# Query projection of a two-layer gated cross-attention kernel: all head pairs in couples, products added in their banks

## What is computed

```python
def _L1_xattn_ref(query, key, value, mask, wq, wk, wv, wo):      # 32 query heads of 128, 8 key heads
    q = (query @ wq).reshape(bs, s, N_Q_HEADS, D_K).transpose(0, 2, 1, 3)
    ...
    q = _rope(q)                                                 # x * cos + rot(x) * sin
    ...
    scores = jnp.einsum('bhgqd,bhkd->bhgqk', qg, k) / scale
    ...
    return out @ wo
x = x + jnp.tanh(g_xattn[1]) * _L1_xattn_ref(_layernorm(x, axis=-1), ctx_4096, ctx_4096, mask_BxSxS2_ff1, ...)
```

## Time and profile before

| | |
|---|---|
| median of 3 runs | 2954.3 us (2952.41 to 2957.29) |
| the profiled execution | 2956.85 us, its span 2955.0 us |
| TensorE (PE) | 2920.1 us busy, 99% |
| VectorE (DVE) | 2138.5 us, 72% |
| ScalarE (ACT) | 1392.4 us, 47% |
| GpSimd (POOL) | 1473.9 us, 50% |
| query projection alone, 979 to 1576 us | PE 588.6 of 597 us, DVE 440.0, ACT 167.9, POOL 455.8 |

### The profile page before, as it was taken

One profiled execution on the slowest core, in us unless ns is written; L12 is line 12 of the kernel. 1 busy time (PEld: TensorE's weight loads), 2 busy tenths in 40 slices (PEclk: granted clock), 3 DMA queues, 4 the chain that ended last, 5 costly groups with the idle time before them and its releaser, 6 DMA issues.

```text
span 2955.0 us, 41425 instructions
## 1 busy us (share of the span) xinstructions
PE 2920.1 (99%) x14509; PEld 2449.0 (83%) x14509; DVE 2138.5 (72%) x4912; ACT 1392.4 (47%) x2906; POOL 1473.9 (50%) x1187
## 2 busy tenths in 40 slices
PE   9999999999999999999999999999999999999999
PEld 7888788887688878878888888888888888888887
DVE  8687788887654876688667877676766676766566
ACT  5555566764332422232224666655555555555332
POOL 0000598984322777778776555544444433333254
PEclk9999999999999999999999999999999999999999
DMA  5533221205464654455444777766577556654531
GB/s 200 155 124 116 79 75 70 79 22 179 157 201 151 197 148 113 109 170 140 108 113 143 232 247 233 244 201 211 187 225 237 182 184 193 195 188 153 228 113 73
DMA packets 299546, 471.14 MB, mean 159 GB/s; under 512 B 25725, under 2 KB 138877, under 8 KB 296525
## 3 DMA queue, kind: packets, MB, share of 16 engines
q1 hardware_dynamic: 298620, 467.06, 50.0%
q10 hardware_dynamic: 720, 1.44, 0.1%
HBM read 323.73 MB, written 144.70 MB: 159 GB/s over the span
## 4 chain that ended last, share of the span: by engine, by line
PE 59%; DVE 4%; POOL 1%; DMA 1%; issue 0%; ACT 0%; SPq 0%; POOLq 0%; DVEq 0%; ACTq 0%
PE PB L150 18%; PE PB L151 18%; PE PB L152 18%; PE PB L2432 4%; DVE qp_b L2166 1%; DMA qp_raw<-in_wq 0%; PE PB L2899 0%; DVE PB L2208 0%; DVE qp_r L2214 0%; DVE qp_r L2205 0%; POOL qp_a L2236 0%; POOL at_ql L2608 0%; DVE at_ss L2579 0%; DVE PB L2190 0%; DVE qp_c L2210 0%
## 5 line engine op out<-in xcount | busy, mean ns | idle before, releaser
L2489 ACT ACTIVATE at_ss<-at_ss,at_sm,at_bs 128x256 f32<-128x256 f32 x512 | 301.9, 591 | 325.1 <-DVE at_sm L2569 325.1
L2608 POOL TENSOR_TENSOR at_ql<-at_qf,at_qh 128x512 fp32r<-128x512 f32 x128 | 166.3, 1300 | 530.4 <-ACT at_qh L2473 530.4
L150 PE MATMUL PB<-at_woh,at_ah 128*128 128x512 f32 x1024 | 400.3, 391 | 0.6 <-DVE at_al L2591 0.6
L151 PE MATMUL PB<-at_wol,at_ah 128*128 128x512 f32 x1024 | 399.8, 390 | 0.0
L152 PE MATMUL PB<-at_woh,at_al 128*128 128x512 f32 x1024 | 398.9, 390 | 0.0
L150 PE MATMUL PB<-qp_b,qp_a 128*128 128x512 f32 x896 | 350.8, 391 | 7.8 <-DVE qp_r L2212 3.2
L2599 DVE SCALAR_TENSOR_TENSOR at_xt<-PB,gt,at_xt 128x512 f32<-128x512 f32 x256 | 192.2, 751 | 225.4 <-PE PB L152 224.3
L151 PE MATMUL PB<-qp_b,qp_a 128*128 128x512 f32 x896 | 349.8, 390 | 0.0
L152 PE MATMUL PB<-qp_b,qp_a 128*128 128x512 f32 x896 | 349.7, 390 | 0.0
L2236 POOL TENSOR_TENSOR qp_a<-qp_raw,qp_a 128x512 fp32r<-128x512 f32 x192 | 259.9, 1365 | 99.4 <-ACT qp_a L2128 96.6
L2128 ACT ACTIVATE qp_a<-qp_raw 128x512 fp32r<-128x512 f32 x192 | 113.4, 626 | 292.7 <-POOL qp_raw L2240 162.4
(11 more groups left out here) (327 smaller groups left out, 7854.2 us busy)
## 6 DMA issues: line engine op xcount, KB each, us to landing
at_woh<-wod SPq DMA_DIRECT2D x48, 1024.0 KB, 7.1
at_wol<-wod SPq DMA_DIRECT2D x48, 1024.0 KB, 9.4
qp_raw<-in_wq SPq DMA_DIRECT2D x32, 1024.0 KB, 5.4
qd<-qp_r SPq DMA_DIRECT2D x256, 128.0 KB, 2.5
at_qf<-qd SPq DMA_DIRECT2D x128, 256.0 KB, 3.4
at_rawo<-in_wo SPq DMA_DIRECT2D x32, 512.0 KB, 5.5
wod<-at_woh SPq DMA_DIRECT2D x16, 1024.0 KB, 5.5
wod<-at_wol SPq DMA_DIRECT2D x16, 1024.0 KB, 6.4
```

The lines of the kernel that those rows point to most:

```text
L150: pe.matmul(o, ah, bh, start=start, stop=False, skip_group_check=onto)
L151: pe.matmul(o, ah, bl, start=False, stop=False, skip_group_check=onto)
L2489: m = act.activation(at_ss[s][:, c, :], at_ss[s][:, c, :], ACT.Exp, bias=z[:, 4 + c:5 + c], scale=at_bs[:, qn % 2, 8 + 2 * b + c % 2:9 + 2 ...
L2608: self.pool.tensor_tensor(at_ql[n % 3][:, :], at_qf[n % 2][:, :], asf(at_qh[n % 3][:, :]), ALU.subtract).then_inc(*inc("at_pool", ("q", n)))
```

## The change

All pairs are now in couples. For all pairs but the last couple (`Q_ADDED`) the sums over products are made by TensorE, which adds one product onto the bank of another: M0, M1, M2 and M5 go to one bank (the sum after M5 is sum 5), M3 and M6 to a second, M4 to a third. What is needed of the stages in between is copied out by ScalarE: M0 to `c11`, M0 + M1 to `c12`, M3 to `c22` (`keep`; it was one copy, inside `sum`, and is now three). VectorE has three additions: `c22 = c22 + (M0 + M1 + M2)` is sum 3, `c11 + M4` sum 4, `c12 + (M3 + M6)` sum 6. So a product that adds onto a bank waits for the copy or the sum that reads it before.

The first two copies of the first couple go ahead of the factors 4 and 5 on ScalarE. `x(1,4)` is made, and `x(1,6)` fetched, after the last products of (14,15) and ahead of its turn 1, where it was before M6. `x(1,0)` and `x(1,1)` are fetched in block (4,5). The second piece of the second attention's start (the mask's preparation on VectorE, three GpSimd operations for the first keys) stands ahead of pair 28 and not 29.

```diff
-        Q_BLOCKS = [(0, 1)] + [(n,) for n in range(2, NP - 2)] + [(NP - 2, NP - 1), (NP, NP + 1)] + [(n,) for n in range(NP + 2, LASTP - 1)] + [
-            (LASTP - 1, LASTP)]
+        Q_BLOCKS = [(n, n + 1) for n in range(0, LASTP, 2)]
+        Q_ADDED = Q_COUPLED[:-2]
...
         def qp_bank(pair, i):
             j = qp_at(pair, i)
+            if pair in Q_ADDED:
+                j = qp_at(pair, 0) + {3: 2, 6: 2, 4: 4}.get(i, 0)
...
+        def qp_goes_on(pair, i):
+            return pair in Q_ADDED and i in (1, 2, 5, 6)
...
         def qp_emptied(pair, i):
+            if pair in Q_ADDED and i < 4:
+                return ("qp_dve", ("sum", pair, 3)) if i == 2 else ("qp_act", ("sum", pair, i))
...
+            for pair in Q_BLOCKS[0]:
+                do.keep(pair, 0)
             for k in range(4, NR - 1):
                 do.prepare(*Q_ORDER[k])
...
-                if block[0] in (NP + 2, LASTP - 2):
+                if block[0] in (NP + 2, LASTP - 3):
                     yield
...
                         do.product(pair, i)
+                        if pair > 1 or i:
+                            do.keep(pair, i)
                         do.sum(pair, i)
...
+                    if block[0] == NP - 2 and i == 6:
+                        do.expand(1, 4)
+                        do.fetch_x(1, 6)
                     if i > 4 and block[-1] < LASTP:
...
-                    if block[0] == 3 and i < 2:
+                    if block[0] == 4 and i < 2:
                         do.fetch_x(1, i)
-                    if block[0] == NP - 2 and i:
+                    if block[0] == NP - 2 and i and i != 5:
                         do.expand(1, i - 1)
...
                         m = three(self.pe, BK[b], (w[:, 0, 2 * k + c, :], w[:, 1, 2 * k + c, :]), (x[:, 0, c, :], x[:, 1, c, :]),
-                                  k + c == 0, k + c == 2)
+                                  k + c == 0 and not qp_goes_on(pair, i), k + c == 2, qp_goes_on(pair, i))
...
-            def sum(self, pair, i):
+            def keep(self, pair, i):
                 if i == 0:
                     self.on.wait_ge(*at("qp_pe", ("M", pair, 0)))
...
+                if pair in Q_ADDED and i in (1, 3):
+                    self.on.wait_ge(*at("qp_pe", ("M", pair, i)))
+                    if i == 3 and pair - 2 in Q_ADDED:
+                        self.on.wait_ge(*at("qp_dve", ("q1", pair - 2, 1)))
+                    self.act.activation((qp_c12 if i == 1 else qp_c22)[pair % 2][:, :], BK[qp_bank(pair, i)], ACT.Copy).then_inc(
+                        *inc("qp_act", ("sum", pair, i)))
...
+            def add(self, pair, i):
+
+                dve, on, m = self.dve, self.on, BK[qp_bank(pair, i)]
+                c11, c12, c22 = (a[pair % 2][:, :] for a in (qp_c11, qp_c12, qp_c22))
+                if i == 3:
+                    on.wait_ge(*at("qp_pe", ("M", pair, 2)))
+                    on.wait_ge(*at("qp_act", ("sum", pair, 3)))
+                    dve.tensor_tensor(c22, c22, BK[qp_bank(pair, 2)], ALU.add).then_inc(*inc("qp_dve", ("sum", pair, 3)))
+                if i == 4:
+                    on.wait_ge(*at("qp_pe", ("M", pair, 4)))
+                    on.wait_ge(*at("qp_act", ("sum", pair, 0)))
+                    dve.tensor_tensor(m, c11, m, ALU.add).then_inc(*inc("qp_dve", ("sum", pair, 4)))
+                if i == 6:
+                    on.wait_ge(*at("qp_pe", ("M", pair, 6)))
+                    on.wait_ge(*at("qp_act", ("sum", pair, 1)))
+                    dve.tensor_tensor(m, c12, m, ALU.add).then_inc(*inc("qp_dve", ("sum", pair, 6)))
```

More of the change, by code:

```diff
@@ L2085, in none @@
                 pass
-            fetch_rope = fetch_w = fetch_x = prepare = expand = product = sum = turn = none
+            fetch_rope = fetch_w = fetch_x = prepare = expand = product = keep = sum = turn = none
         class QpTensor(Queries):
@@ L2172, in sum @@
                 c11, c12, c21 = (a[pair % 2][:, :] for a in (qp_c11, qp_c12, qp_c21))
+                if pair in Q_ADDED:
+                    self.add(pair, i)
+                    return
                 if i == 0:
@@ L2198, in turn @@
                     on.wait_ge(*at("qp_rope", 1))
-                    on.wait_ge(*at("qp_dve", ("sum", pair, (5, 6)[tn])))
+                    if pair in Q_ADDED and tn == 0:
+                        on.wait_ge(*at("qp_pe", ("M", pair, 5)))
+                        on.wait_ge(*at("qp_dve", ("sum", pair, 4)))
+                    else:
+                        on.wait_ge(*at("qp_dve", ("sum", pair, (5, 6)[tn])))
                     if n > 1:
```

## The result

The changed kernel takes **2963.47 us** (median of 7 runs, 2961.02 to 2965.53) where the kernel before took 2955.14 on the same chip (7 runs, 2951.95 to 2957.38): a ratio of 1.0029, 95% interval 1.0019 to 1.0038. It is 8.3 us slower, where +1.7 was forecast. That is 1.5 us outside the forecast's own range (2949 to 2962), inside the wider one that counts half of a rival (2945 to 2966), and beyond the 0.2% that can be told from no change.

A forecast was written before the change was run, and what follows sets the result against it. TensorE, busy 99% of the span, was taken to bound the kernel, with at most 11.7 us to win. 3.5 - 4.2 + 9.2 - 7.5 + 0.7 = +1.7 us on 2954.3 gave 2956.0 us, range 2949 to 2962.

The forecast's parts named there:

- half of a rival: The wider range for the whole kernel with half of either rival on the forecast's side: 2945 to 2966 us.
- first couple: Pairs 0 to 3: waits for ScalarE's copies and pair 3's weights, 3.5 us with restarts where 4.2 went before.
- steady couples: Couples away from the making of activations: ScalarE's copy of M0 comes in time, so no wait, 0.
- second activations: Pairs 16 and 17: ScalarE's copies late behind the second activations' factors, 9.2 us where 7.5 went before.
- start of the attention: Four GpSimd operations that PE waits for at 1577.62, beside pair 29's turn 1: +0.7 us, bounds -0.2 and +1.5.
- slack 3.1: In steady couples, ScalarE's copy of M0 was put 3.1 us ahead of when it is wanted.
- the rival of stalls at every couple: ScalarE's copy of M0 late at each of 13 changes of couple: 2965, or 2978 with 1 us more each; chance 0.14.
- into a place where POOL was idle 47.9 of 195 us: The second attention's prepared pieces, moved one pair earlier on GpSimd and VectorE, were to cost nothing.
- VectorE: Whole kernel: 83 us of additions gone, 57 us of slower turns added, so about 26 us less busy.
- ScalarE: Whole kernel: 60 copies of 0.60 us, so 36 us more busy.
- The first rival: Waits at both activation places go: half gone wins 5.3 us (2949), all gone 11.7 (2942.5); chance 0.2.
- the rival's half case: Half of the forecast's waits at the two activation places gone: 5.3 us won, 2949 us.

The follow-up runs named there:

- e12: The kernel before, nothing added and its own blocks, with only the fastest version's order of the second activations: 2953.70 us, ratio 0.9999.
- e2: The changed kernel with sum 3 of pairs 28 and 29 in free PSUM banks in place of SBUF: 2959.29 us, ratio 1.0013.
- e3: The changed kernel with the second piece of the attention's start ahead of pair 26 in place of 28: 2960.74 us, ratio 1.0014.
- e11: The changed kernel with sum 3 in banks, the attention's piece ahead of pair 26, and the copies and turns 0 ahead of the second activations' factors: 2950.95 us, 0.9981.
- couples-alone kernel: The kernel before with all pairs in couples and the attention's piece ahead of pair 28, nothing added in banks: 2966.08 us, ratio 1.0032.

## Why the prediction was right or wrong

By place, the lost time in us (idle, 0.26 for each restart, and the slow stretch behind, counted over 4 us as in the prediction):

| | before | forecast | measured |
|---|---|---|---|
| first couple | 4.2 | 3.5 | 1.25 + 1.64 + 0.46 + 0.8 = 4.1 |
| steady couples | 0 | 0 | 0 |
| second activations | 7.5 | 9.2 | 1.07 + 4.26 + 1.52 + 0.8 + 1.3 = 8.9 |
| start of the attention, over before | | +0.7 | +3.0, and +1.5 behind it |
| change in all | | +1.7 | +5.8 |

- **First couple.** The copy of M0 + M1 was 1.25 late (1.3 forecast, 1.6 with the restart), at the place forecast. The weights of pair 3 were 1.64 late, where I had 0.7, and the copy behind them 0.46 instead of 0.8. Right, 0.6 short. That 4.2 went in exchange holds for the profiled execution only, as e12 shows.
- **Steady couples, slack 3.1.** Right: no wait in 190 us. ScalarE had waited 1.87 us for M0 before its copy at 1104.04, and that copy had another 2.72 - 0.60 to spare, so the slack was 4.0; the rival of stalls at every couple has nothing for it.

```profile
1104.04 0.60 ACT L2171 ACTIVATE qp_c<-PB 128x512 f32<-128x512 f32 x1 [1.87 <-PE PB L152]
```

- **Second activations.** Right in mechanism: ScalarE's copies behind `expand`, with a slow stretch behind the larger wait (12 matmuls in 4.0 us, at least 1.3 lost). That the sum is only 0.3 off is in part luck. The waits were 4.3 and 1.5 where I had 3.4 and 4.4 with their restarts. The slow stretch, which I had behind the second for 1.4, came behind the first and ran while `x(1,6)` was awaited. ScalarE had `x(1,6)` at 1309.04, 2 us later than I put it (0.6 of them the later start of the stage), and ahead of all stood a wait of 1.07 for pair 17's weights, which I did not have at all. What was too much and what was missing nearly cancel.
- **The end is the step that failed**: "bounds are -0.2 and +1.5 ... I take +0.7". It cost 3.0 of wait and 1.5 of slow clock. The mechanism was named, but its size was taken from three turn instructions of pair 29 at 0.5 each, beside four GpSimd operations. There were six such instructions, pair 28's too, beside eight operations in the queue ahead of the keys, and these lost 2.6 us (e2). And "into a place where POOL was idle 47.9 of 195 us ... nothing" was wrong: the attention's prepared piece delayed factor 6 and the fetch of weights behind it, on an engine whose whole queue ends at that wait (e3). A wait that grows from 1.3 to 4.4 us also brought a slow stretch that 1.3 had not.
- **VectorE** went down by 38, not 26. The single pairs are 24 and not 26 (2 to 13 and 18 to 29), so by the prediction's own prices the turns cost 53 and not 57, and 30 was the forecast to make. And turn operations with two SBUF inputs took 1.20, 1.27 and 1.19 on average in the steady couples, not 1.45, 1.65 and 1.17. The ten turns that I had read all lay in couples of the kernel before; that those in the steady part met GpSimd less often is what the averages suggest, not a run of its own. **ScalarE** went up by 33.5 for 36.

The rest up to 8.3 us is 0.6 ahead of the stage and 1 behind 1655, where neither kernel differs in code, and the spread of a profiled execution against a median. Its cause stays open.

The first rival ("the waits go") did not come true in this kernel. In e11, with other banks and another order, the attention does start 5.2 us earlier, near the rival's half case of 5.3; but that is another kernel.

## What to carry to other kernels

Where TensorE is busy 99% of the time, additions taken from a hidden engine are worth nothing in the steady part; what counts is the queue order at the seams, where rare long work (here the factors of the activations) stands ahead of short work that TensorE waits for. Each wait mended showed the next one under it, so a mend that moves the time little may still be right. Of the versions tried only the one with order, banks, piece and adding together was faster than before; neither the adding nor the order was so alone. Whether it needs every one of them was not tried: the last order was run neither with single pairs and adding, nor without the banks for sum 3. Before a result is left in SBUF to save a bank, look at what GpSimd does beside it, through its whole queue up to the next thing that TensorE needs.

## What had not been expected of the hardware

GpSimd loses as well as VectorE when VectorE reads two inputs from SBUF: four like operations took 6.43 us for 5.08. Over the whole kernel GpSimd is 27 us busier. These are the groups of GpSimd in the steady couples, 1060 to 1255 us (operation, count, busy us, mean ns, idle before), where the first had a mean of 1294 and the second one of 1296 before:

```profile
L2281 POOL TENSOR_TENSOR qp_a<-qp_raw,qp_a 128x512 fp32r<-128x512 f32 x63 | 84.4, 1354 | 24.9 <-ACT qp_a L2143 23.6
L2281 POOL TENSOR_TENSOR qp_a<-qp_s,qp_a 128x512 fp32r<-128x512 f32 x10 | 16.2, 1627 | 0.6 <-ACT qp_a L2143 0.4
```

In the traces of ten kernels with such a wait, the low clock stood behind, or from within, every projection wait of 2.9 us or more (granted clock 0.50 to 0.63 over the 4 to 8 us behind it, between the levels 2.4 and 1.2 GHz). Below, the length of the wait does not decide: 2.65 in the kernel before had none, 2.25 and 2.15 had it, and of those from 1.0 to 1.8 one had it, 1.80 at 1027.15 in the couples-alone kernel (0.57 over 1028 to 1032), while 1.74 at the same place in e11 had not. The count of 12 matmuls in 4.0 us gives 1.3 us as the price:

```profile
1298.00:1302.00 4.00, 4.00 (x11) 3.18 (x12) 3.93 (x7) 2.78 (x4) 3.73 (x3) 0.60 0.59 208
```

(such a stretch, with 11 begun, in the couples-alone kernel). Counted to the end of the low clock it is more. In the changed kernel the 23 steps behind 1302.72 took 6.96 us where 23 x 0.227 is 5.2, which is 1.6 beside the longer first row; where the low clock lasted longer, in e2, 23 steps behind 1300.90 took 8.01, 2.8 more. So a wait of 4 us costs 6 to 7, and cutting it to 1 gives back more than the 3 us by which it is shorter.
